# Audio tower with routed experts: all first weights resident, sums fetched by token number, tiles scattered into the output

## The chip, the cores and the metric

The kernel runs on one core of one Trainium2 chip. The time is the device time of one execution in microseconds (us), and lower is better. Times of the unchanged kernel are the median of three runs. The engines are named as in the profile: PE is TensorE (matmuls; PEld is its weight load), DVE is VectorE, ACT is ScalarE, POOL is GpSimd, SP is SyncE, which here only issues DMAs. A "q" behind an engine's name is its queue of instructions other than computing ones.

## What is computed

The input is 64 signals of 4000 samples. Seven strided convolutions of 128 channels, each with a layernorm over the channels and an exact gelu, leave 12 tokens for each signal, 768 tokens in all. A projection takes them to 192 values, an attention with 6 heads inside each signal of 12 tokens is added, and last a layer with 9 experts:

```
xt = layernorm(h).reshape(-1, 192)
route_prob = softmax(xt @ Ws + bs)
p, routes = max(route_prob), argmax(route_prob)
h1 = gelu(einsum('td,edf->tef', xt, W1) + b1)
out = einsum('tef,efd->ted', h1, W2) + b2
common = out[:, 0, :]
sel = out[token, routes[token], :]
final = where(routes == 0, common, p * sel + (1 - p) * common)
return h + final
```

W1 is 9 x 192 x 768, W2 is 9 x 768 x 192, all float32. Expert 0 is computed for every token (the common part). Experts 1 to 8 are computed only for the tokens that chose them.

## The kernel before

All five engines have a program of their own, written out by hand, and meet in semaphores. The signals are worked in 8 groups (`NT`) of 8. A table of slots (`SLOTS`, lines 121 to 218) sets which chunk of which convolution and which side job stands in a slot, and every engine walks that same table. The tokens of a group are worked 16 to 22 slots behind its last convolution (`STEP_AT`, `TIGHT`). The last slots (`DRAIN`) hold the last group's chunks, its attention and the common expert's jobs "up" and "down". Behind the table come `AFTER` = down(6), up(3), down(7).

What matters here is what follows the last convolution:

- **Choice.** For each group DVE finds the chosen expert and each token's place among that expert's tokens; POOL scatters the 96 rows, with the token's number as 193rd element, by an indirect DMA into the DRAM table `sorted_tokens` (line 623), which has a region for each expert. When the last group is placed, DVE works out in 13 short steps (lines 1255 to 1270) which expert owns each of the 13 tiles (`owni`) and at which row it starts (`rowi`). `s_own` tells of both.
- **Tiles.** `NTILE` is 13 and a tile is 128 rows. SP reads an owner and starts that expert's W1 and its row of b1 (lines 535, 536) into one of `WR` = 3 buffers: 576 KB. Two of these lie in the stream buffer h[1][0] and one in `xhl`. It then loads the tile's tokens (line 542) into one of `XR` = 4 buffers. Its order is weights 0 to 2, tokens 0 to 3, then weights j and tokens j+1 in turn. Weights j wait for up(j-3), and tokens j wait until tile j-4 is stored.
- PE turns the 128 x 192 tokens (lines 969, 970), multiplies with W1 (lines 981, 982: 24 instructions), and after ACT's gelu (line 1431) with W2 (line 993: 12 instructions). W2 of all experts lies in SBUF from early on. PE's order is turn(j+2), up(j+1), down(j). DVE copies the turned tokens (`take`, line 1292) and adds the chosen bias (`result`, line 1299). POOL stores the tile by an indirect DMA into the DRAM table `chosen_results` (line 696) and, before each store, waits for the one before it.
- **End.** When all tiles are stored, SP loads `chosen_results` back in four parts (line 557), DVE adds p times it to `acc` (line 1317, 8 instructions), and SP writes four parts of the output (line 561). `acc` holds h plus (1-p) times the common part; lines 1279 to 1312 make it between tiles 1 and 2.

W1 of expert 0 (`W1c`) is loaded at the start. The biases `b2s` are loaded by SP when the last convolution is done (line 527).

## Time and profile before

| | us |
|---|---|
| median of 3 runs | 646.53 (645.88 to 650.91) |
| the profiled execution, its own time | 646.93 |
| its span, first to last instruction | 645.1 |
| last convolution chunk starts on PE | 496.0 |
| last down job of the common expert ends on PE | 550.7 |
| first turn of a tile starts on PE | 555.0 |
| last result of a tile starts on DVE | 633.0 |
| busy in the span: PE, DVE, ACT, POOL | 569.5, 315.0, 301.8, 277.0 |

The profiled execution lies 0.4 us above the median, and 1.8 us of it lie outside the span. The page's busy shares are means over stages of different kinds: up to about 496 us the convolutions stream through all engines, from there to 551 us one group's attention and choice run as a chain of small steps, from 551 to 633 us the 13 tiles run, and the rest is the end. Only the last two stages and what feeds them are touched by the change, so a reader has to look at stretches and not at the totals.

### The profile page before, as it was taken

What the parts mean: (1) busy time and instruction counts of PE and PEld (TensorE: products, weight loads), DVE (VectorE), ACT (ScalarE), POOL (GpSimd) and SP (SyncE); (2) the same over time, 40 slices, a digit from 0 to 9 for tenths busy, and PEclk for the clock granted to TensorE, in tenths of its full rate; (3) what the DMA queues carried; (4) which work ended last, traced back from release to release, by engine and by line L of the source; (5) the groups of instructions that cost most, each with busy time, mean ns of one, the idle gap of its engine ahead of it and who ended that gap; (6) DMA issues with size and microseconds to landing.
All of it is one profiled execution on the core that took longest, in us unless ns stands there. A gap on an engine that the chain in (4) does not pass through costs nothing.

```text
span 645.1 us, 11944 instructions
## 1 busy us (share of the span) xinstructions
PE 569.5 (88%) x4499; PEld 538.3 (83%) x4499; DVE 315.0 (49%) x736; ACT 301.8 (47%) x494; POOL 277.0 (43%) x410
## 2 busy tenths in 40 slices
PE   6877899989989999998999999899997787687882
PEld 6776899989989989998998999889986666687882
DVE  4653465455657566665756666555544233131112
ACT  1545466746655674665567466546434132011110
POOL 4573285794267429526742952343322101011111
PEclk9998999999999999999999999999999756799997
DMA  6290000790000000000000000000001001544532
GB/s 181 71 269 9 3 1 10 170 228 24 2 1 10 8 1 1 6 1 2 1 6 2 1 7 1 1 1 6 2 6 54 6 1 43 133 103 108 142 105 85
DMA packets 19403, 29.21 MB, mean 45 GB/s; under 512 B 1916, under 2 KB 14567, under 8 KB 19349
## 3 DMA queue, kind: packets, MB, share of 16 engines
q1 hardware_dynamic: 16853, 19.97, 11.3%
q0 software_dynamic: 2480, 8.49, 5.5%
q8 instruction: 37, 0.61, 0.4%
q14 instruction: 17, 0.14, 0.1%
q10 hardware_dynamic: 16, 0.00, 0.0%
HBM read 19.38 MB, written 9.08 MB: 44 GB/s over the span
## 4 chain that ended last, share of the span: by engine, by line
PE 66%; POOL 8%; DMA 7%; ACT 7%; DVE 6%; issue 4%; SPq 1%; DVEq 0%; POOLq 0%; ACTq 0%
PE ps L738 36%; PE ps L750 5%; DMA chosen_results<-h 4%; PE ps L803 3%; POOL rstd L596 3%; POOL rstd L605 2%; PE ps L824 2%; DMA h<-sorted_tokens 2%; PE ps L993 2%; ACT h L1368 2%; ACT sq L1339 2%; PE ps L864 2%; PE ps L981 2%; PE ps L794 2%; PE ps L982 2%
## 5 line engine op out<-in xcount | busy, mean ns | idle before, releaser
L738 PE MATMUL ps<-wt,h 128*128 128x128 f32 (+2 forms) x2496 | 301.7, 276 | 16.0 <-ACT h L1368 9.0
L738 PEld LDWEIGHTS ps<-wt,h 128*128 128x128 f32 (+2 forms) x2496 | 290.9, 189 | 21.2 <-issue 13.1
L1339 ACT ACTIVATE sq<-ps 128x512 f32<-128x512 f32 (+7 forms) x128 | 67.3, 526 | 184.3 <-PE ps L738 184.0
L605 POOL TENSOR_TENSOR rstd<-varv,neghalf 128x4 f32<-128x4 f32 (+7 forms) x128 | 117.0, 914 | 10.0
L1068 DVE TENSOR_REDUCE ssum<-sq 128x4 f32<-128x512 f32 (+7 forms) x128 | 75.5, 590 | 87.5 <-ACT sq L1339 87.4
L1078 DVE TENSOR_TENSOR xh<-ps,rstd 128x512 f32<-128x512 f32 (+7 forms) x128 | 76.3, 596 | 82.8 <-POOL rstd L605 82.7
L1357 ACT ACTIVATE h<-ps,lncol 128x512 f32<-128x512 f32 (+7 forms) x128 | 112.8, 881 | 5.9 <-PE ps L750 5.3
L602 POOL TENSOR_TENSOR varv<-ssum,ceps 128x4 f32<-128x4 f32 (+7 forms) x128 | 26.2, 205 | 204.5 <-DVE ssum L1068 204.2
L596 POOL TENSOR_TENSOR rstd<-var,half 128x10 f32<-128x10 f32 (+2 forms) x39 | 82.8, 2131 | 9.4 <-DVE var L1034 9.4
L1368 ACT ACTIVATE h<-ps,lncol 128x512 f32<-128x512 f32 (+1 forms) x120 | 82.0, 727 | 2.2 <-PE ps L803 2.2
L750 PE MATMUL ps<-ident,xh 128*128 128x128 f32 (+2 forms) x424 | 66.3, 270 | 6.7 <-ACT h L1357 5.5
L750 PEld LDWEIGHTS ps<-ident,xh 128*128 128x128 f32 (+2 forms) x424 | 49.5, 141 | 9.6 <-issue 6.9
L696 POOL DMA_INDIRECT chosen_results<-h x13 | 12.5, 964 | 81.0 <-DVE h L1299 78.9
L803 PE MATMUL ps<-xcol,w0t 120*128 120x512 f32 (+1 forms) x120 | 43.3, 424 | 2.1 <-DVE xcol L1055 0.8
L1431 ACT ACTIVATE h<-ps 128x768 f32<-128x768 f32 x13 | 10.5, 811 | 70.9 <-PE ps L982 70.9
L1299 DVE TENSOR_TENSOR h<-ps,wt 128x192 f32<-128x192 f32 x13 | 4.7, 358 | 50.2 <-PE ps L993 50.2
L993 PE MATMUL ps<-W2s,h 128*128 x156 | 27.3, 326 | 0.0
L1055 DVE CAST xcol<-ps 120x512 fp32r<-120x512 f32 (+1 forms) x40 | 25.1, 628 | 1.4 <-PE ps L794 1.3
L993 PEld LDWEIGHTS ps<-W2s,h 128*128 128x128 f32 x156 | 25.1, 190 | 0.0
L824 PE MATMUL ps<-W2s,h 128*96 128x192 f32 x96 | 23.8, 415 | 0.4 <-ACT h L1374 0.4
L803 PEld LDWEIGHTS ps<-xcol,w0t 120*128 120x128 f32 x120 | 19.6, 190 | 5.2 <-ACT h L1368 2.5
L794 PE MATMUL ps<-ident,xhl 128*120 128x128 f32 x144 | 22.4, 273 | 1.3 <-DVE xhl L1048 1.2
(208 smaller groups left out, 655.8 us busy)
## 6 DMA issues: line engine op xcount, KB each, us to landing
sorted_tokens<-zero POOLq DMA_DIRECT2D x1, 5886.5 KB, 32.2
W2s<-in_L_ffn_W_dram SPq DMA_DIRECT2D x9, 576.0 KB, 8.4
h<-in_L_ffn_W_dram SPq DMA_DIRECT2D x9, 576.0 KB
xhl<-in_L_ffn_W_dram SPq DMA_DIRECT2D x4, 576.0 KB
h<-sorted_tokens SPq DMA_DIRECT2D x13, 96.5 KB, 2.0
xnat<-in_x_dram SPq DMA_DIRECT2D x7, 135.0 KB
wt<-in_L_ffn_b_dram SPq DMA_DIRECT2D x1, 864.0 KB, 4.0
h<-in_L_tok_conv_w_dram SPq DMA_DIRECT2D x4, 192.0 KB, 3.9
```

What stands on the lines that cost most here:

```text
L596: gp.tensor_tensor(rstd0[:, lo:hi], var0[:, lo:hi], half0[:, lo:hi], ALU.pow).then_inc(s_pow, 1)
L605: gp.tensor_tensor(rstd[0:rows, idx, 0:count], varv[0:rows, idx, 0:count], neghalf[0:rows, 0:count], ALU.pow).then_inc(rstd_done, 1)
L738: last = nc.tensor.matmul(y[0:rows, j * C:(j + 1) * C], src, wt[:, TAP0[l] + tap, :], start=(tap == 0), stop=(tap == taps - 1))
L750: last = nc.tensor.transpose(tr[:, j * rows:(j + 1) * rows], xh[0:rows, n % 2, j * C:(j + 1) * C], ident[0:rows, 0:rows])
L803: nc.tensor.matmul(o[:, 0:w], w0t[:, j, :], xcol[q % 2][0:12 * K0, 0:w], start=True, stop=True).then_inc(j_done, 1)
L824: last = nc.tensor.matmul(o[0:M, 0:D], hc[:, f, i * M:(i + 1) * M], W2s[:, 0, f, :], start=(f == 0), stop=(f == NF - 1))
L993: last = nc.tensor.matmul(o, ht[:, b, f * P:(f + 1) * P], W2s[:, bass.ds(own, 1), f, :].rearrange("p e d -> p (e d)"), start=(f == 0), sto ...
L1068: nc.vector.reduce_sum(ssum[0:rows, n % 4, 0:count], sq[0:rows, n % 2, 0:w].rearrange("p (j c) -> p j c", c=C), axis=X).then_inc(ssum_done, 1)
L1078: nc.vector.tensor_tensor(xh[0:rows, n % 2, 0:w].rearrange("p (j c) -> p j c", c=C), ybank(n)[0:rows, 0:w].rearrange("p (j c) -> p j c", c=C),
L1339: nc.scalar.activation(sq[0:rows, n % 2, 0:w], ybank(n)[0:rows, 0:w], ACT.Square).then_inc(sq_done, 1)
L1357: nc.scalar.activation(dst, src, ACT.Gelu, bias=lncol[:, 8 + l:9 + l], scale=lncol[:, l:l + 1]).then_inc(act_done, 1)
L1368: nc.scalar.activation(dst, src, ACT.Gelu, bias=lncol[:, 8:9], scale=lncol[:, 0:1]).then_inc(j_act, 1)
```

## The change

Six things, in the order of the program:

1. **Memory.** The stream buffers of the convolutions become one tensor `wide`, with W1 of expert 0 ahead of them. `W1s` is a view of it that holds W1 and b1 of all 9 experts. Buffers that lay in the stream buffers move: `ht` to `work` (which held `sq` and `xh`), `xs` to `cols` (which held `xcol`), `ysb` to `xnat`. `XR` is 5 and `YB`, the number of result and sum buffers, is 4.
2. **Weights.** Behind the last convolution SP loads W1 of experts 1 to 8 with 8 DMAs (4.6 MB) and b1 with two. The 13 loads by owner are gone.
3. **Pick.** For each tile ACT copies the owner's 97 x 1536 values from `W1s` to one of two buffers (`xhl`, `watt`), from which PE multiplies. The matmuls, their number and their shapes stay.
4. **Tokens.** SP loads tokens j when `take(j-5)` has copied that buffer's token numbers to `idt`.
5. **Common part.** DVE makes the shares and `acc` ahead of tile 0, around down(7), and not between tiles 1 and 2. `acc` has a 193rd element, p. POOL then writes `acc` to the DRAM table `common_sums` and its first 192 elements to the output, and fetches the first 4 tiles' rows of `common_sums` by token number.
6. **Result.** DVE multiplies the chosen bias by p and adds the fetched sum, and then adds p times PE's result to that: two instructions. `result(j-2)` stands behind `take(j+2)`. PE's down tile goes round three banks. POOL scatters the finished rows into the output itself (rows without a token are left out by the bounds check), waits only for the store four tiles back, and fetches the sums for tile j+4. The load of `chosen_results`, the last 8 additions and the output's four DMAs are gone, and so is the early DMA that cleared `chosen_results`; `common_sums` has its last 128 rows cleared instead.

```diff
+XR = 5
+YB = 4
+        wide = sb("wide", [P, 2 * DFF + 2 * sum(ODD[l] + EVEN[l] for l in range(1, 6))])
+        W1s = wide[0:DH + 1, 0:2 * DFF * NE].rearrange("p (e k c) -> p e k c", e=NE, k=2)
...
+        W1r = [xhl[:, :, :].rearrange("p l k -> p (l k)")[0:DH + 1, 0:2 * DFF], watt[:, :]]
...
# SP
             sp.dma_start(b2s, bass.AP(a["L0_ffn_b2"].tensor, 0, [[0, P], [1, NE * D]])).then_inc(s_b2, 16)
+            for e in range(1, NE):
+                sp.dma_start(W1s[0:DH, e, :, :], a["L0_ffn_W1"][e].rearrange("(k p) n -> p k n", p=DH)).then_inc(s_w1, 16)
+            for k in range(2):
+                sp.dma_start(W1s[DH:DH + 1, 1:NE, k, :], a["L0_ffn_b1"][1:NE, :].rearrange("(a e) n -> a e n", a=1)).then_inc(s_w1, 16)
             sp.wait_ge(s_own, 2)
+            sp.wait_ge(s_sent, 16 * NT)
...
                 if j >= XR:
-                    sp.wait_ge(s_ys[(j - XR) % 2], 16 * ((j - XR) // 2 + 1))
+                    sp.wait_ge(e_ids, j - XR + 1)
...
-            for i in range(0, NT, 2):
-                sp.dma_start(sel[:, i:i + 2, :], ys_dram[i * M:(i + 2) * M, :].rearrange("(i p) d -> p i d", p=M)).then_inc(s_got[i // 2], 16)
...
# POOL
+            def fetch_sums(j):
+                gp.wait_ge(e_ids, j + 1)
+                gp.indirect_dma_start(out=sums[:, j % YB, :], out_offset=None,
+                                      in_=sum_dram[:, :], in_offset=ids(j)).then_inc(s_got[j % YB], 16)
+            gp.wait_ge(c_acc, NT)
+            gp.dma_start(sum_dram[0:TOKENS, :].rearrange("(i p) d -> p i d", p=M), acc[:, :, :]).then_inc(s_sums, 16)
+            gp.dma_start(out_rows.rearrange("(i p) d -> p i d", p=M), acc[:, :, 0:D]).then_inc(s_out, 16)
+            gp.wait_ge(s_sums, 16)
+            for j in range(YB):
+                fetch_sums(j)
+            gp.wait_ge(s_out, 16)
             for j in range(NTILE):
                 gp.wait_ge(e_res, j + 1)
-                if j >= 1:
-                    gp.wait_ge(s_ys[(j - 1) % 2], 16 * ((j - 1) // 2 + 1))
+                if j >= YB:
+                    gp.wait_ge(s_ys[j % YB], 16 * (j // YB))
+                gp.indirect_dma_start(out=out_rows, out_offset=ids(j), in_=ysb[:, j % YB, :], in_offset=None,
+                                      bounds_check=TOKENS - 1, oob_is_err=False).then_inc(s_ys[j % YB], 16)
+                if j + YB < NTILE:
+                    fetch_sums(j + YB)
# DVE
+                ve.wait_ge(s_got[b], 16 * (j // YB + 1))
+                nc.vector.scalar_tensor_tensor(out=sums[:, b, 0:D], in0=b2s[:, bass.ds(own * D, D)], scalar=sums[:, b, D:D + 1],
+                                               in1=sums[:, b, 0:D], op0=ALU.mult, op1=ALU.add).then_inc(s_mix, 1)
...
+                nc.vector.scalar_tensor_tensor(out=ysb[:, b, :], in0=ps[:, 4 + j % 3, 0:D], scalar=sums[:, b, D:D + 1],
+                                               in1=sums[:, b, 0:D], op0=ALU.mult, op1=ALU.add).then_inc(e_res, 1)
...
                 if j + 2 < NTILE:
                     take(j + 2)
-                result(j)
+                if j >= 2:
+                    result(j - 2)
# ACT
+            def pick(j):
+                own = ac.value_load(owni[0:1, j:j + 1], min_val=0, max_val=NE - 1)
+                nc.scalar.copy(W1r[j % 2], W1s[:, bass.ds(own, 1), :, :].rearrange("p e k c -> p (e k c)")).then_inc(e_pick, 1)
+            ac.wait_ge(s_own, 1)
+            ac.wait_ge(s_w1, 16 * (NE + 1))
+            pick(0)
+            ac.wait_ge(t["at"], NT)
+            pick(1)
             for j in range(NTILE):
                 hidden(j)
+                if j + 2 < NTILE:
+                    pick(j + 2)
```

ACT's program, from its last common gelus to the end, before (h_0 and ps are the tile's hidden values and PSUM):

```order
L1374 ACTIVATE h<-ps 128x96 x6
L1431 ACTIVATE h_0<-ps 128x768 x13
L275 UNCONDITIONAL_BRANCH
```

and the same place now, with the two copies ahead of the first gelu and the first behind it (`wide` holds all experts' W1, `xhl` and `watt` the picked one):

```order
L1396 ACTIVATE h<-ps 128x96 x6
L1457 TENSOR_LOAD owni
L1457 ISA x2
L1458 ISA
L1458 COPY xhl<-wide 97x1536
L1457 TENSOR_LOAD owni
L1457 ISA x2
L1458 ISA
L1458 COPY watt<-wide 97x1536
L1453 ACTIVATE work<-ps 128x768
```

Between two gelus there now stand an owner's load and a copy of 1536 values a partition.

POOL's program from its last scatter of sorted tokens on, before:

```order
L623 DMA sorted_tokens<-xn,sloti 7808x193
L696 DMA chosen_results<-h_0 896x192 x13
L275 UNCONDITIONAL_BRANCH
```

and now, down to the third store:

```order
L620 DMA sorted_tokens<-xn,sloti 7808x193
L696 DMA common_sums<-acc 96x8x193
L697 DMA out_dram<-acc 96x8x192
L691 DMA h<-common_sums,idt 128x193 x4
L706 DMA out_dram<-xnat,idt 768x192
L691 DMA h<-common_sums,idt 128x193
L706 DMA out_dram<-xnat,idt 768x192
L691 DMA h<-common_sums,idt 128x193
```

Two whole stores and four fetches come ahead of the first tile's store, and a fetch stands behind each of the first nine.

SP's program at its end, before:

```order
L535 DMA h_0<-in_L_ffn_W_dram 96x2x768
L536 ISA
L536 DMA h_0<-in_L_ffn_b_dram 1x768
L557 DMA h<-chosen_results 96x2x192 x4
L561 DMA out_dram<-acc 96x2x192 x4
L275 UNCONDITIONAL_BRANCH
```

and now from the biases on, where the weights come ahead of the first tokens:

```order
L540 DMA wt<-in_L_ffn_b_dram 128x1728
L542 DMA wide<-in_L_ffn_W_dram 96x2x768 x8
L544 DMA wide<-in_L_ffn_b_dram 1x8x768 x2
L549 TENSOR_LOAD rowi
L549 ISA x2
L552 ISA
L552 DMA cols<-sorted_tokens 128x193
```

SP has nothing behind the last tile's tokens but the waits for the stores.

## Rows read from the trace of the kernel before

**Rows 1.** The chain that ended last, and waits from 550 us: total, times, longest.

```profile
PE 66%; POOL 8%; DMA 7%; ACT 7%; DVE 6%; issue 4%; SPq 1%; DVEq 0%; POOLq 0%; ACTq 0%
...
PE ps L969 <- DMA h<-sorted_tokens: 14.4, 10, 4.4
```

**Rows 2.** Stretches: length, busy us (count) of PE, PEld, DVE, ACT, POOL; clock, DMA share, GB/s.

```profile
551.00:560.80 9.80, 5.09 (x28) 4.72 (x29) 0.88 (x3) 0.00 (x0) 0.00 (x0) 0.65 0.38 94
560.80:633.00 72.20, 62.02 (x468) 59.04 (x467) 12.61 (x38) 10.54 (x13) 11.57 (x12) 1.00 0.42 110
```

**Rows 3.** Timeline of several engines, 496 to 569 us: start, length, engine, instruction.

```profile
496.59 0.37 SPq L527 DMA_DIRECT2D wt<-in_L_ffn_b_dram  x1
...
541.24 0.96 POOL L623 DMA_INDIRECT sorted_tokens<-xn,sloti  x1 [5.71 <-DVE sloti L1177]
...
548.10 0.25 ACT L1374 ACTIVATE h<-ps 128x96 f32<-128x96 f32 x1 [0.24 <-PE ps L815]
...
550.69 0.35 DVE L1059 TENSOR_TENSOR h<-ps,b2c 96x192 f32<-96x192 f32 x1 [5.94 <-PE ps L824]
...
555.01 0.42 PE L969 MATMUL ps<-ident,h 128*96 128x128 f32 x1 [4.35 <-DMA h<-sorted_tokens]
...
556.77 0.63 PE L981 MATMUL ps<-xst,h 96*128 96x128 f32 x2
...
563.76 2.12 PE L993 MATMUL ps<-W2s,h 128*128 x12
...
568.61 2.12 PE L993 MATMUL ps<-W2s,h 128*128 x12
```

**Rows 4.** Pieces of the chain that ended last: start, length, what.

```profile
543.84 0.48 SPq L531
...
544.83 0.35 SPq L535
...
557.40 0.43 PE ps L982 x2
...
567.17 2.38 DMA chosen_results<-h
...
569.71 1.97 DMA h<-sorted_tokens
...
572.15 0.22 PE ps L981 x2
...
574.83 1.97 PE ps L993 x12
```

**Rows 5.** Timeline of DVE, POOL and SP, 571 to 645 us.

```profile
571.15 0.21 DVE L1279 TENSOR_REDUCE r<-lgb 96x8 f32<-96x72 f32 x1
...
572.62 2.72 DVE L1312 SCALAR_TENSOR_TENSOR acc<-h,c,acc 96x192 f32<-96x192 f32 x8
...
631.09 0.36 DVE L1299 TENSOR_TENSOR h<-ps,wt 128x192 f32<-128x192 f32 x1 [4.27 <-PE ps L993]
...
633.04 0.36 DVE L1299 TENSOR_TENSOR h<-ps,wt 128x192 f32<-128x192 f32 x1 [1.59 <-PE ps L993]
...
637.15 1.81 SPq L557 DMA_DIRECT2D h<-chosen_results  x4
```

**Rows 6.** The chain's piece for the last but one store.

```profile
631.72 2.32 DMA chosen_results<-h
```

**Rows 7.** Groups on ACT by shape: count, busy us, mean ns, idle before.

```profile
L1396 ACT ACTIVATE t<-t 96x576 f32<-96x576 f32 x8 | 5.5, 684 | 0.1
...
L1431 ACT ACTIVATE h<-ps 128x768 f32<-128x768 f32 x13 | 10.5, 811 | 70.9 <-PE ps L982 70.9
```

**Rows 8.** DMA issues: engine, count, KB each, median us to landing.

```profile
sorted_tokens<-zero POOLq DMA_DIRECT2D x1, 5886.5 KB, 32.2
...
wt<-in_L_ffn_b_dram SPq DMA_DIRECT2D x1, 864.0 KB, 4.0
```

**Rows 9.** A stretch of PE: length, busy, granted clock, DMA share, GB/s.

```profile
505.00:506.00 1.00, 0.17 (x2) 0.55 0.00 0
```

More of the change, by code:

```diff
@@ L33 @@
 ROWS = (NE - 1) * REGION + NTILE * P
-WR = 3
-XR = 4
+XR = 5
+YB = 4
 SEG = 16
@@ L396, in audio_tower @@
         xs_dram = nc.dram_tensor("sorted_tokens", [ROWS, D + 1], F32, kind="Internal").ap()
-        ys_dram = nc.dram_tensor("chosen_results", [TOKENS + P, D], F32, kind="Internal").ap()
+        sum_dram = nc.dram_tensor("common_sums", [TOKENS + P, D + 1], F32, kind="Internal").ap()
+        out_rows = out.rearrange("b t d -> (b t) d")
         ps = ctx.enter_context(nc.psum_tensor("ps", [P, 8, 512], F32))
@@ L459, in audio_tower @@
         s_sent = sem("tokens_sorted")
-        s_w1 = [sem(f"first_weights_here{k}") for k in range(WR)]
+        s_w1 = sem("first_weights_here")
         s_xs = [sem(f"tile_tokens_here{k}") for k in range(XR)]
+        e_pick = sem("tile_weights_picked")
         e_turn = sem("tile_turned")
+        e_ids = sem("tile_numbers_kept")
         e_copy = sem("tile_copied")
@@ L1270, in _ @@
             nc.vector.tensor_copy(rowi[:, :], rowf[:, :]).then_inc(s_own, 1)
-            for job in AFTER:
-                if job[0] == "down":
-                    job_down(job)
             def shares():
```

126 lines of the change are left out of this document (60 added, 66 removed).

## The prediction

> **What bounds the kernel now.** I read the chain that ended last first. PE holds 66% of it, but that is a mean over the whole program [rows 1]. So I cut the end into stretches [rows 2]. Up to 551 us the change touches nothing on the chain; behind that come three parts.
>
> - From 551.0 to 560.8 us PE is busy 5.1 of 9.8 us at a mean clock of 0.65 [rows 2]. The last down job is taken by DVE at 550.69 to 551.04, but PE turns the first tile only at 555.01, after 4.35 us that end with a DMA of sorted tokens [rows 3]. SP had three experts' weights to issue ahead of the tokens: its owner is read at 543.84 and the first weights start at 544.83 [rows 4]. The tokens queue behind 1.7 MB.
> - From 560.8 to 633.0 us PE is busy 62.0 of 72.2 us at full clock [rows 2]. Ten times it waits for tokens, 14.4 us in all with the 4.4 us of the first [rows 1], so 10.0 us inside the loop. The chain tells why: store of a tile 2.38 us, then tokens 1.97 us [rows 4]. Tokens j wait for the store of tile j-4, which shares the DMA engines with 576 KB of weights.
> - Where tokens were in time, two tiles follow each other at PE's own pace: W2 matmuls start at 563.76 and 568.61 [rows 3], a period of 4.85 us. It is made of up, 2.68 us (572.15 to 574.83), down, 1.97 us [rows 4], and 0.2 us for the turn.
> - From 633.04 to the end at 645.1 us PE has nothing to do: result, two stores in a row, loads back at 637.15, additions, output [rows 5].
>
> **The change part by part**, against this execution's span of 645.1 us.
>
> *Weights early.* SP may start them at 496.59, where the biases go today [rows 3]. Price: 4.72 MB. The biases' 864 KB landed in 4.0 us and the clearing of 5886 KB in 32.2 us [rows 8], so 216 and 183 KB a us, or 22 to 26 us. They are in by 525 us, and ACT wants them at 548.35, the end of its last common gelu [rows 3]. 23 us are to spare. PE waits on small steps meanwhile, and only the scatters share the DMA engines, so I cost it at nothing. Upper end: 1 us, if the small scatters or the engines' instruction fetch are held up.
>
> *Start of the tiles.* SP can issue the first tokens 1.0 us after 543.84 [rows 4]; 1.97 us later they are there, at about 547. The last scatter starts at 541.24 [rows 3] and is in before. Even at twice that price the tokens are early, so what is late next is down(7) on DVE, 551.04. DVE's new work ahead of it: down(6), shares, seven additions. From 571.15 to 572.62 seven of the short steps take 1.5 us and eight additions 2.72 us [rows 5]; now eight steps and seven additions, 1.7 + 2.4 = 4.1 us, start at about 544.7 and end at 548.8, before the down job. The eighth addition, 0.35 us, lies beside PE's first turn. So turn 0 starts at 551.15. Today 1.76 us lie between it and up(0) (555.01 to 556.77) at half clock [rows 3]; at full clock I take 1.35. up(0) starts at 552.5, not 556.77.
>
> *Clock of up(0).* Two matmuls took 0.43 us in it, and 0.22 us later on [rows 4]. Now PE pauses only 0.5 us before the turns, not 4.35. I take full clock: up(0) ends at 555.2 and the first W2 matmul starts 2.9 us later (turn, up(1)), at 558.1, against 563.76. That is 5.65 us saved.
>
> *Pick.* An ACT copy of 1536 values from SBUF stands nowhere in this trace. 576 values from SBUF took 0.684 us and 768 from PSUM 0.811 [rows 7]. Scaled by length alone these give 1.8 and 1.6 us; with a fixed part of 0.2 us, 1.4 to 1.5. Bounds 1.4 and 1.9; I take 1.5. The owner's load before it costs 1.0 us at most, as on SP [rows 4]. Ready: 548.35 + 2.5 = 550.9 for tile 0, before 552.5; 553.4 for tile 1, before 555.4. In the loop ACT has 0.81 + 1.0 + 1.5 = 3.3 us of work in 4.85. The tightest is tile 2: its copy waits for up(0)'s end, 555.2, is ready at 558.6, and PE wants it at 560.3. PE hides it; without cover it costs its excess over 1.7 us once, and over 1.5 us on each tile.
>
> *Sums.* The last addition ends at 551.45. POOL issues two stores of 0.59 MB, an issue 0.9 to 1.0 us as for the scatter [rows 3]. At 183 KB a us [rows 8] each moves in 3.2 us; with 2 us until it is noticed, `common_sums` is whole at about 558, at the latest 561 where both share. The first fetch lands 2.4 to 4 us on, at 560 to 565. Who waits: `result(0)` stands behind `take(4)`, at about 565; behind it stand `take(5)`, for which PE asks at 574.7, and PE's down(3) at 572.6. So 7 us are to spare for PE. Nothing is added.
>
> *Loop.* DVE per tile: take, number copy, two additions of 0.41 at most [rows 5], an owner's load of 1.0 us: 2.5 us. POOL: a store and a fetch, 0.96 each plus 0.3 before each: 2.5 us. Tokens now wait for a copy of numbers five tiles back, 20 us early. All lie under 4.85. From 558.1: ten periods, 48.5; one without turn, 4.65; the last two downs, 3.95. End of PE at 615.2. Today the same takes 563.76 to 633.0, 69.3 us; now 57.1. That is 12.15 us saved.
>
> The Trainium skill has a rule that speaks against this (SBUF — State Buffer, section 'SBUF: two separate sides'): a VectorE operation with two SBUF inputs and a GpSimd operation that reads SBUF take a port pair in turn and block each other for a whole instruction. The new bias addition is such a one. By that rule DVE's 2.5 us grow by up to 0.96 to 3.5, and POOL's by 0.4; the sum stays and the third rival gets a little more. The trace has additions of that kind beside no DMA issue, so it shows nothing of it.
>
> *End.* Today 12.05 us behind 633.04. Now: the last addition 0.41, 0.3 to the store (631.09 + 0.36 to 631.72 [rows 5, 6]), the store 2.32 [rows 6], and 0.4 for the closing of the engines: 3.4 us. POOL's former wait for the store before is gone. 8.65 us saved.
>
> **Sum.** 5.65 + 12.15 + 8.65 = 26.45. Span 645.1 - 26.45 = 618.65, and 1.8 us outside it: 620.5 us for such an execution. This one lay 0.4 us above the median of 646.53; I leave that for the small costs taken as nothing. Forecast 620.5.
>
> **Rivals.**
>
> 1. *The clock falls at the seam or inside the loop.* For: it went down around 505 us in a pause of about 2 us (mean 0.55 in that stretch) [rows 9], and PE has two pauses of about 0.5 us at the seam. Against: in the loop pauses of 1.0 us a tile left it at 1.00 throughout [rows 1, 2]. Price: up(0) and part of up(1) at half clock, as from 556.77 on: 1.3 us, to 2.9 if the turns and a whole further round go slow. 620.5 + 2.5 = 623 us. The Trainium skill (TensorE: Matmul & The Clock Gate, section 'A second HAM failure mode: psum-queue depth-cycling') says that short idle times between groups of matmuls can make the clock swing; by that rule this rival would be likelier than the loop's 1.00 makes it.
> 2. *The sums are late.* If the store of 0.59 MB took as long as the large clearing, 32.2 us [rows 8], they would be there at 584, the first rows at 587, and PE, stopped at 572.6, would lose 15 us: 636 us. Against: the clearing moved ten times the bytes.
> 3. *A helper becomes the bound of a tile.* ACT, if a copy takes over 3.0 us with its load at 1.0, or DVE with loads and blocked ports. At half a us over on each of 13 tiles: 627 us. Against: the upper bound of 1.9 us from [rows 7] leaves 1.1 us.
> 4. *Slower than before.* Each store and fetch on POOL is generated by that engine. If a fetch of 128 rows of 772 B costs far more than the scatter's 0.96 us [rows 3], POOL sets the pace. It takes 26.5 us over 13 tiles, so 4.85 + 2.04 = 6.9 us a tile, to reach today's time: a fetch of over 5.3 us. At 6 us the time is 656 us. For: no gather stands in this trace. Against: a scatter of rows as long is the same work the other way.
>
> **How the numbers follow.** Forecast 0.72 (618.5 to 622.5 by its own bounds: copy, closing, seam), rival 1 0.12, rival 3 0.08, rival 2 0.05, rival 4 0.03. The range goes from 618.0, where the small steps turn out cheaper, to 626.5: it takes in rival 1 and part of 3 and leaves out some 0.15. A measurement of this kernel tells from no change about 1%, 6.5 us. Rivals 1 to 3 are all faster than that, so faster 0.96, within 1% 0.01, slower 0.03.
>
> **What would show it.** Right: first turn at about 551.2 us with no wait for tokens; PE's W2 groups 4.85 us apart throughout, clock 1.00 from there on; ACT's copies near 1.5 us; PE's last matmul at about 615 us and the end under 4 us behind; weights landed by 525 us. Wrong: PE waiting for the pick, a mean clock under 0.9 from 551 to 561 us, DVE waiting for fetched sums past 566 us, POOL's fetches well over 1 us, or a longer stretch from 500 to 551 us, where the weights now move.

## The result and the profile after

The changed kernel took 627.02 us (median of four runs, 622.12 to 628.29) where the kernel before, on the same chip, took 648.72 us (645.88 to 651.43). The ratio is 0.966, interval 0.962 to 0.970. The forecast was 620.5 us in a range of 618.0 to 626.5, so the sign and most of the size came out, and the median lies 0.5 us above the range. Five later runs of the same program on another occasion (E1) gave 621.99 us and a ratio of 0.961.

The profiled execution took 628.29 us, with a span of 626.6 us and a mean granted TensorE clock of 0.953. Its span against that of before and the prediction, cut at four places that all traces have. The third row, from the last down job of the common expert to the first W2 matmul of a tile, is called the seam below:

| stretch | before | predicted | after | E1 |
|---|---|---|---|---|
| start to SP's load of the biases (last convolution done) | 496.59 | 496.59 | 501.52 | 497.65 |
| to DVE's last common down job | 54.10 | 54.10 | 54.19 | 51.81 |
| to the first W2 matmul of a tile | 13.07 | 7.41 | 7.37 | 7.36 |
| to DVE's last result | 69.28 | 57.10 | 57.54 | 57.50 |
| to the end | 12.06 | 3.45 | 5.98 | 5.98 |
| span | 645.1 | 618.65 | 626.6 | 620.3 |

Each number is the start of a row minus the start of the row before it: before, 496.59, 550.69, 563.76 and 633.04 us [rows 3, 5]; after, 501.52, 555.71, 563.08 and 620.62 us, all shown below. Two of the five rows differ from what was predicted: the first, by 4.9 us, and the last, by 2.5 us. Together with 0.5 us in the loop they make the 8 us by which the span is longer than forecast.

The chain's shares by engine, from the page of the profile after, and PE's longest waits (total, times, longest):

```profile
PE 74%; POOL 8%; ACT 7%; DVE 6%; issue 4%; DMA 1%; SPq 1%; POOLq 0%; DVEq 0%; ACTq 0%
...
PE ps L750 <- ACT h L1390: 9.0, 5, 2.7
```

Against [rows 1] DMA fell from 7% of the chain to 1%. The wait for tokens, 14.4 us before, is gone from the list; the longest that PE has now are for ACT's gelus in the head of the program, the convolutions' part up to the load of the biases, which will matter below.

The two stretches of [rows 2], in the columns given there:

```profile
551.00:560.80 9.80, 8.17 (x63) 7.48 (x62) 4.63 (x16) 4.52 (x8) 1.67 (x2) 0.99 0.45 110
...
560.80:615.00 54.20, 54.20 (x428) 53.84 (x428) 14.39 (x45) 24.61 (x23) 22.63 (x23) 1.00 0.22 61
```

PE is busy 54.20 of 54.20 us where it was busy 62.0 of 72.2, and the mean clock of the first stretch is 0.99, not 0.65. The share of the DMA engines in the loop fell from 0.42 to 0.22.

The timeline of after from the end of the convolutions on, the places of [rows 3]:

```profile
501.52 0.37 SPq L540 DMA_DIRECT2D wt<-in_L_ffn_b_dram  x1
501.93 4.40 SPq L542 DMA_DIRECT2D wide<-in_L_ffn_W_dram  x8
...
551.37 2.39 DVE L1305 SCALAR_TENSOR_TENSOR acc<-h,c,acc 96x192 f32<-96x192 f32 x7
...
554.04 1.47 ACT L1458 COPY xhl<-wide 97x1536 f32 x1 [0.67 <-issue]
...
555.71 0.35 DVE L1071 TENSOR_TENSOR h<-ps,b2c 96x192 f32<-96x192 f32 x1 [1.95 <-PE ps L836]
...
556.17 0.28 PE L981 MATMUL ps<-ident,cols 128*96 128x128 f32 x1 [0.49 <-issue]
...
557.14 0.88 POOL L696 DMA_DIRECT2D common_sums<-acc  x1 [9.92 <-DVE acc L1305]
...
557.50 0.39 PE L993 MATMUL ps<-xst,xhl 96*128 96x128 f32 x2
...
563.05 1.04 POOL L691 DMA_INDIRECT h<-common_sums,idt  x1 [4.25 <-DMA common_sums<-acc]
...
563.08 2.12 PE L1005 MATMUL ps<-W2s,work 128*128 x12
...
567.93 2.12 PE L1005 MATMUL ps<-W2s,work 128*128 x12
...
571.33 0.42 DVE L1312 SCALAR_TENSOR_TENSOR h<-wt,h 128x192 f32<-128x192 f32 x1 [0.56 <-issue]
```

Read from top to bottom: the weights start when the convolutions end; DVE's seven additions take 2.39 us and are over at 553.76, 1.95 us before the last common job; ACT's copy takes 1.47 us and is done at 555.51, before PE asks for it at 557.50; PE turns the first tile 0.46 us after that last job started on DVE, where it used to turn it 4.32 us after it; and the W2 groups lie 4.85 us apart. The fetched sums are issued at 563.05 and used at 571.33, with nobody waiting.

The end of after: the timeline of DVE and POOL, the last pieces of the chain (start, length, what), and the closing of POOL's program (durations in ns, start):

```profile
620.62 0.42 DVE L1318 SCALAR_TENSOR_TENSOR xnat<-ps,h 128x192 f32<-128x192 f32 x1 [1.00 <-PE ps L1005]
621.83 0.98 POOL L706 DMA_INDIRECT out_dram<-xnat,idt  x1 [1.21 <-DVE xnat L1318]
```

```profile
621.07 0.03 POOLq L706
621.10 0.51 issue
621.61 1.21 POOLq L275
```

```profile
L275 POOLq DRAIN  x1: 4715/4715/4715, 621.6 to 621.6; - x1
```

The store starts 0.79 us behind the result, and not the 0.27 of before. Then POOL's closing instruction, which begins at 621.61, ends only at 626.33, 3.5 us behind the end of the store's issue at 622.81. That is the end of the program. In the trace of before the same instruction is there too:

```profile
L275 POOLq DRAIN  x1: 3718/3718/3718, 634.6 to 634.6; - x1
```

It began at 634.58 and ended at 638.30, 2.5 us behind the issue that ran from 634.80 to 635.76. The reload of the results lay over it, so it cost nothing, and the prediction, which allows 0.4 us for the closing of the engines, did not count it.

### The profile page after: what moved, and what is told of

Read it like the earlier page. It is cut to its first block, busy times and chain, and to the rows that moved or that the text cites. A ratio compares the mean times of both kernels' runs of the same rounds, so it can differ in the third digit from the quotient of the medians.

```text
span 626.6 us, 11944 instructions
## 1 busy us (share of the span) xinstructions
PE 572.0 (91%) x4499; PEld 542.5 (87%) x4499; DVE 319.8 (51%) x755; ACT 320.0 (51%) x507; POOL 291.6 (47%) x425
## 4 chain that ended last, share of the span: by engine, by line
PE 74%; POOL 8%; ACT 7%; DVE 6%; issue 4%; DMA 1%; SPq 1%; POOLq 0%; DVEq 0%; ACTq 0%
PE ps L750 38%; PE ps L762 5%; PE ps L1005 4%; PE ps L836 3%; PE ps L815 3%; POOL rstd L593 3%; PE ps L994 3%; PE ps L993 3%; POOL rstd L602 2%; ACT h L1390 2%; ACT work L1361 2%; PE ps L876 2%; PE ps L806 2%; ACT wide L1379 2%; PE ps L896 1%
## 5 line engine op out<-in xcount | busy, mean ns | idle before, releaser
L750 PE MATMUL ps<-wt,h 128*128 128x128 f32 x1248 | 155.3, 282 | 10.0 <-ACT h L1390 9.0
L1361 ACT ACTIVATE work<-ps 128x512 f32<-128x512 f32 (+7 forms) x128 | 67.3, 525 | 188.4 <-PE ps L750 188.1
L750 PEld LDWEIGHTS ps<-wt,h 128*128 128x128 f32 x1248 | 150.2, 198 | 11.8 <-issue 6.5
L750 PE MATMUL ps<-wt,wide 128*128 128x128 f32 (+2 forms) x1248 | 150.5, 274 | 5.6 <-ACT wide L1379 5.4
L750 PEld LDWEIGHTS ps<-wt,wide 128*128 128x128 f32 (+2 forms) x1248 | 144.6, 184 | 9.0 <-issue 6.1
L1080 DVE TENSOR_REDUCE ssum<-work 128x4 f32<-128x512 f32 (+7 forms) x128 | 75.6, 590 | 91.6 <-ACT work L1361 91.5
L1090 DVE TENSOR_TENSOR work<-ps,rstd 128x512 f32<-128x512 f32 (+7 forms) x128 | 76.4, 597 | 82.8 <-POOL rstd L602 82.7
L1379 ACT ACTIVATE wide<-ps,lncol 128x512 f32<-128x512 f32 (+6 forms) x120 | 109.3, 911 | 2.3 <-PE ps L762 1.6
L762 PE MATMUL ps<-ident,work 128*128 128x128 f32 (+2 forms) x424 | 66.9, 272 | 6.5 <-ACT wide L1379 5.5
L762 PEld LDWEIGHTS ps<-ident,work 128*128 128x128 f32 (+2 forms) x424 | 50.2, 143 | 9.1 <-issue 6.9
```

What stands on the lines that cost most here:

```text
L750: last = nc.tensor.matmul(y[0:rows, j * C:(j + 1) * C], src, wt[:, TAP0[l] + tap, :], start=(tap == 0), stop=(tap == taps - 1))
L762: last = nc.tensor.transpose(tr[:, j * rows:(j + 1) * rows], xh[0:rows, n % 2, j * C:(j + 1) * C], ident[0:rows, 0:rows])
L1080: nc.vector.reduce_sum(ssum[0:rows, n % 4, 0:count], sq[0:rows, n % 2, 0:w].rearrange("p (j c) -> p j c", c=C), axis=X).then_inc(ssum_done, 1)
L1090: nc.vector.tensor_tensor(xh[0:rows, n % 2, 0:w].rearrange("p (j c) -> p j c", c=C), ybank(n)[0:rows, 0:w].rearrange("p (j c) -> p j c", c=C),
L1361: nc.scalar.activation(sq[0:rows, n % 2, 0:w], ybank(n)[0:rows, 0:w], ACT.Square).then_inc(sq_done, 1)
L1379: nc.scalar.activation(dst, src, ACT.Gelu, bias=lncol[:, 8 + l:9 + l], scale=lncol[:, l:l + 1]).then_inc(act_done, 1)
```

## The experiments

Times are medians over the executions of a kernel; stretches and rows are those of its one profiled execution. The ratio is always to the kernel before, run on the same chip in the same session.

### E1: the changed kernel again

> The changed kernel unchanged, five rounds. Theory (the 6.5 us by which the forecast was missed are 4.9 us of TensorE's clock ahead of the change's stages and 2.5 us of the end): single runs fall into steps, about 622 us where the mean granted clock is 0.968, 626 at 0.960, 628 at 0.953, so time falls with the clock, some 0.4 us for each 0.001, and kernel before shows the same steps (646 to 651). Rival (the moved buffers or the early weights cost 5 us in every execution): times of the changed kernel do not follow the clock, and no run is below 624.

Measured: 621.99 us (five runs, 620.75 to 623.38, clock 0.965 to 0.971) against 647.46 us in the same session, ratio 0.9614 (0.9584 to 0.9643). The rival, no run below 624 us, is out. Over all nine executions the time goes with the clock, as the theory has it: 628.2 and 628.3 us at 0.953, 625.85 at 0.960, 623.4 at 0.965, 622.0 to 622.1 at 0.968, 620.8 to 620.9 at 0.971. The table above has its stretches. The three that the change is about agree with those of after within 0.04 us; the first two are 3.9 and 2.4 us shorter. So the same program varies by 6 us between these two profiles, and all of it lies ahead of the seam. The next runs ask whether TensorE's clock makes this difference.

### E2 and E3: the three pauses of the head filled, in the changed kernel and in the one before

```diff
+HEADFILL = {(1, 0, 5): 7, (1, 1, 0): 7, (1, 1, 1): 8}
...
+            def fill(k, bank):
+                for _ in range(k):
+                    nc.tensor.matmul(ps[:, bank, 0:P], ident[:, :], ident[:, :], start=True, stop=True)
             def conv(chunk):
...
+                if chunk in HEADFILL:
+                    fill(HEADFILL[chunk], n % 3)
```

> The changed kernel with 7, 7 and 8 matmuls without use put into the three pauses of PE at 42 to 64 us (ahead of chunks (1,0,5), (1,1,0), (1,1,1)); each takes about 0.22 us at full clock, 1.5 to 1.8 us in a pause of 2.2 to 2.7. Theory: the clock stays at 1.00 from 45 to 70 us, the 4 us lost there come back, times gather at 621 to 624 us with less spread. Rival (it isn't the pause): clock and times as without them, 622 to 628, or up to 1 us longer where the fill outlasts a pause.

> The same three fills in the kernel before. Theory: 640 to 645 us, less spread than 645.9 to 651.4, and the difference to the filled changed kernel is 23.5 to 24.5 us (26.45 as predicted, less 2.5 of the end). Rival: times as before, 646 to 651.

PE has three pauses of 2.2 to 2.7 us near 45, 55 and 64 us. The convolution of 24 matmuls behind each of them shows the clock by its length. Timeline of PE, before, and then after:

```profile
45.34 2.92 PE L738 MATMUL ps<-wt,h 128*128 128x128 f32 x24 [2.36 <-ACT h L1368]
...
54.23 4.54 PE L738 MATMUL ps<-wt,h 128*128 128x128 f32 x24 [2.18 <-ACT h L1368]
...
62.57 2.92 PE L738 MATMUL ps<-wt,h 128*128 128x128 f32 x24 [2.65 <-ACT h L1368]
```

```profile
44.83 4.43 PE L750 MATMUL ps<-wt,h 128*128 128x128 f32 x24 [2.35 <-ACT h L1390]
...
55.35 4.54 PE L750 MATMUL ps<-wt,h 128*128 128x128 f32 x24 [2.19 <-ACT h L1390]
...
63.69 5.46 PE L750 MATMUL ps<-wt,h 128*128 128x128 f32 x24 [2.66 <-ACT h L1390]
```

The pauses are the same in both, and the work too. Before, one of the three convolutions ran for the most part at the lower of the clock's two levels (1.2 and 2.4 GHz); after, all three. Set against before at the same instruction of POOL, after is 0.5 us early at 44 us, 3.7 us late at 67 us and still 3.7 us late at 493 us. The last 1.2 us of the 4.9 come just ahead of the load of the biases, where after's clock is 0.50 to 0.53 from 497 to 500 us: four matmuls of 288 columns (L826, L827 of after) take 2.05 us there, and 1.32 before. The stretch from 15 to 70 us (length, then busy us of PE, PEld, DVE, ACT, POOL, clock, DMA share, GB/s), in after, and then in E2:

```profile
15.00:70.00 55.00, 44.18 (x298) 40.82 (x297) 25.64 (x60) 26.44 (x39) 27.31 (x24) 0.88 0.37 107
```

```profile
15.00:70.00 55.00, 48.44 (x387) 44.91 (x386) 27.95 (x63) 29.14 (x43) 29.44 (x28) 1.00 0.37 108
```

Measured: E2 620.85 us (618.84 to 621.93), ratio 0.960 (0.957 to 0.963), just under the 621 to 624 expected; E3 644.69 us (641.43 to 647.5, twelve runs), ratio 0.995 (0.993 to 0.998). With the pauses filled the clock from 15 to 70 us is 1.00 in E2, and its load of the biases starts at 494.06 us, against 501.52 in after. In the four profiled executions with filled pauses (E2, E3, E4, E10) all twelve convolutions take 2.94 us; in the ten without, 21 of 30 take 4.2 to 5.5 us. What follows: the head of the changed kernel is not slower as such; unfilled, it ended between 496.24 and 501.66 us in the nine profiled executions of kernels with the new layout (after, E1, E5, E6, E8, E9, E11 to E13), and before's 496.59 lies near the lower end of that.

Filling is worth about 1 us to E1's median and 3 us to the median before. It does not remove the whole spread of the head. An earlier place, from 17 to 27 us, was left unfilled in every run: PE pauses twice for 0.83 us there, and the clock from 15 to 30 us is 0.77 in E4 and E8, 0.89 in E1, E3 and E5, and 1.00 in the other nine. E4's head therefore ends at 497.03 us, though its three convolutions are at full clock, and E3's at 495.76.

The difference of the medians of E3 and E2, where neither has a slow convolution at 45 to 64 us, is 23.8 us, inside the 23.5 to 24.5 expected. The three stretches of the table, 5.70 + 11.74 + 6.08, make 23.5 of it; those of E3 and E2 themselves make 23.2.

### E4 and E10: the later pauses filled as well

E4 keeps the fills of the head and adds unused matmuls to eight steps of the last group between 500 and 541 us. E10 leaves out one of these steps (turn_norm_h) and adds one more of the last group (scores), two of the group before, the last common up job and the first turns.

```diff
 # E4
+LATEFILL = {'turn_norm_h': 5, 'turn_1': 6, 'turn_probs': 5, 'values': 3, 'turn_heads': 1, 'turn_2': 8, 'logits': 1, 'rank': 4}
...
+                if r == NT - 1 and step in LATEFILL:
+                    fill(LATEFILL[step], 0)
 # E10
+LATEFILL = {('turn_2', 6): 6, ('rank', 6): 6, ('turn_1', 7): 6, ('scores', 7): 1, ('turn_probs', 7): 5, ('values', 7): 3, ('turn_heads', 7): 1, ('turn_2', 7): 8, ('logits', 7): 1, ('rank', 7): 4}
...
+                if (step, r) in LATEFILL:
+                    fill(LATEFILL[step, r], 0)
...
+                if job == ("up", 3, 2):
+                    fill(5, 0)
...
+            fill(2, 0)
             pe.wait_ge(j_dve, DVE_TO[len(JOBS)])
             turn_tile(0)
+            fill(2, 0)
```

> The changed kernel with the head filled and, for the last group alone, 1 to 8 matmuls without use ahead of eight steps for which PE waits (500 to 551 us, where the clock is at half for most of the time). Theory: the clock stays high in more of that stretch, the last group's chain of PE pieces shortens by 5 to 12 us: 611 to 618 us. Rival (the fills outlast the pauses at half clock and the clock falls all the same): 0 to 5 us longer than the head filled alone.

> The changed kernel with matmuls of two 128 x 128 identity tiles, whose results nobody reads, put into every pause of PE that the trace shows as long: the three in the head, the chain of small steps of the last two groups, the last common up job, and the start of the tiles. The output is unchanged. My theory is that what is left of the spread (620.8 to 623.4 us of the same program) is the granted clock, so with the pauses filled the time should be about 615.5 us (614 to 618) with a mean clock over 0.985, under e4's 618.34 because e4 still had low stretches at 500 and 541 us. The rival, that the low clock is not tied to PE's pauses, gives 618 to 622 us with low stretches at the same places. If the unused matmuls themselves delay work on the chain, the times would not fall under e4's fastest, 614.87 us, though the clock is full.

E4 gave 618.34 us (614.87 to 622.64), ratio 0.955 (0.952 to 0.958), 0.3 us above the 611 to 618 expected. Its profiled execution, the slowest of the six, had a low stretch from 541.2 to 554.9 us that reaches across the seam into the first up. In the other profiled executions that have the new layout and their tokens in time, the first up runs at full clock. Window and one matmul pair of the first up:

```profile
541.20:554.90 13.70, 12.07 (x49) 10.54 (x49) 3.59 (x13) 3.78 (x5) 2.70 (x3) 0.50 0.46 130
```

```profile
549.10 0.63 PE L1004 MATMUL ps<-xst,xhl 96*128 96x128 f32 x2
```

So rival 1 of the prediction exists: the first up at half clock. From the last common job (546.88) to the first W2 matmul (557.45) E4 took 10.57 us, against 7.37: 3.2 us, a little over the upper end of 2.9 that the rival was given. What PE did before the fall: it paused for 1.31 us ahead of 539.11, worked on, and from 541.16 its matmul pairs take 0.63 to 0.70 us and not 0.36 to 0.46.

The rule of the Trainium skill that stood beside that rival (TensorE: Matmul & The Clock Gate, section 'A second HAM failure mode: psum-queue depth-cycling'), that short idle times between groups can make the clock swing, is borne out at one place: behind the two pauses of 0.83 us at 17 to 21 us the same convolution takes 4.68 us in E4 and 2.84 in after. The loop, at 1.00 in all kernels with tokens in time, gives no sign of it, and the falls at 45 to 64 us stand behind longer pauses.

E10 gave 611.94 us (610.48 to 616.03), ratio 0.946 (0.941 to 0.950), the fastest version of all: 10 us under E1, with the output unchanged. Its windows:

```profile
496.00:541.70 45.70, 39.25 (x275) 35.97 (x276) 20.29 (x75) 14.16 (x28) 4.91 (x10) 0.93 0.51 136
541.70:606.90 65.20, 63.46 (x496) 62.64 (x495) 17.14 (x52) 26.18 (x25) 26.65 (x28) 1.00 0.22 61
```

The stretch from the biases' load to the last common job takes 46.44 us (494.43 to 540.87) where after took 54.19, and its clock is 0.93 instead of the 0.65 in this row of after:

```profile
501.50:555.70 54.20, 40.75 (x187) 35.55 (x187) 20.39 (x75) 13.69 (x29) 5.64 (x12) 0.65 0.45 115
```

The seam, the loop and the end stay at 7.34, 57.30 and 5.99 us. I had expected 615.5, so the fills were worth 3.6 us more than I gave them. They take no wait away, so what they work on is the clock. The length of the same stretch goes with its mean clock in these profiles: 54.1 to 54.3 us at 0.65 (before, after, E2, E12), 51.8 to 52.2 at 0.70 or 0.71 (E1, E6, E13), 49.85 at 0.84 (E4), 46.44 at 0.93. What these later fills would give the kernel before was not run.

### E5: tokens wait for the store again

```diff
                 if j >= XR:
-                    sp.wait_ge(e_ids, j - XR + 1)
+                    sp.wait_ge(s_ys[(j - XR) % YB], 16 * ((j - XR) // YB + 1))
```

> The changed kernel, but tokens j wait again for the store of tile j-5 and not for the copy of its token numbers. Theory (the wait on the store made the stops of the loop, and late results make it worse): from the first turn of tile k+4 on, DVE's two additions, 0.9 us to the store, 2.4 us for it and 2.1 us for the tokens make 7.4 us against a period of 4.85, so 2.5 us on each of 8 tiles: 642 us, and PE waits for tokens. Rival (only the weights' traffic made the stops): 622 us as without it.

Measured: 645.84 us (642.97 to 648.71), ratio 0.995 (0.992 to 0.999). PE's wait for tokens is back, and the chain shows one turn of the loop:

```profile
PE ps L981 <- DMA cols<-sorted_tokens: 14.8, 7, 3.0
```

```profile
594.46 2.08 DMA cols<-sorted_tokens
...
598.25 0.43 DVE xnat L1318
...
598.74 0.77 issue
599.51 3.02 DMA out_dram<-xnat,idt
```

The loop takes 80.0 us (559.87 to 639.88), longer than the 69.3 of before although the weights' traffic is gone and the store waited for is one tile older. By the chain, the reason is the new order on DVE: a result now comes two tiles behind its turn, so its store is later by as much. The old order with the new weights, E9 below, takes 61.39 us in the loop. The two edits belong together: without the wait for the copied numbers the delayed results would have cost 22.5 us in the loop. Waits of up to 3 us also took the clock down inside the loop (0.51 from 604 to 611 us), which is part of it; the expectation was 642.

### E6: the weights only when the owners are known

```diff
+            sp.wait_ge(s_own, 2)
             for e in range(1, NE):
...
-            sp.wait_ge(s_own, 2)
             sp.wait_ge(s_sent, 16 * NT)
```

> The changed kernel, but SP starts the 4.7 MB of weights only when the owners are known, and not at the last convolution. Theory (the early place hides 20 us of transfer): weights start at about 544 instead of 502 us (by a profile whose first tile turns at 551), land 19 to 20 us on, the first up tile starts near 567 instead of 552.5: 637 us; the stretch up to 545 stays the same within 0.5 us, since early weights cost nothing there. Rival (early weights slow the attention of the last group): that stretch gets 1 us or more shorter.

Measured: 644.2 us (641.47 to 650.98), ratio 0.995 (0.990 to 1.000), 7 us more than I had said. ACT waits for the last weights, and PE for tokens queued behind them. Timeline of ACT and of PE, and the window of the low clock:

```profile
566.27 0.42 PE L981 MATMUL ps<-ident,cols 128*96 128x128 f32 x1 [17.72 <-DMA cols<-sorted_tokens]
...
566.74 1.47 ACT L1458 COPY xhl<-wide 97x1536 f32 x1 [20.49 <-DMA wide<-in_L_ffn_b_dram]
```

```profile
552.60:573.00 20.40, 5.92 (x26) 5.15 (x27) 0.96 (x4) 2.84 (x2) 2.02 (x2) 0.50 0.74 212
```

From DVE's last common job (548.59) to the first W2 matmul (576.27) it is 27.7 us, 20.3 more than in E1. 17.2 of them are the longer wait for tokens (17.7 against 0.5 us), and 3.1 come from half clock in the first two up jobs (566.27 to 576.27 is 10.0 us, against 6.91 in after). With its weights loaded late the kernel gives back 22 of 25.5 us. The early transfer itself costs the stretch that it lies beside nothing that shows at equal clock: 54.19 us with it (after) and 54.10 without (before), both at 0.65, and 52.13 with it (E13) and 52.24 without (E6), both at 0.71.

### E9: memory, early weights and pick alone

The kernel before with parts 1 to 3 of the change; tokens, common part, result and end as they were.

```diff
+            for e in range(1, NE):
+                sp.dma_start(W1s[0:DH, e, :, :], a["L0_ffn_W1"][e].rearrange("(k p) n -> p k n", p=DH)).then_inc(s_w1, 16)
...
-            for j in range(WR):
-                load_weights(j)
             sp.wait_ge(s_sent, 16 * NT)
-            for j in range(XR):
+            for j in range(NTILE):
                 load_tokens(j)
-            for j in range(WR, NTILE):
-                load_weights(j)
-                if j + 1 < NTILE:
-                    load_tokens(j + 1)
...
+            def pick(j):
+                own = ac.value_load(owni[0:1, j:j + 1], min_val=0, max_val=NE - 1)
+                nc.scalar.copy(W1r[j % 2], W1s[:, bass.ds(own, 1), :, :].rearrange("p e k c -> p (e k c)")).then_inc(e_pick, 1)
```

> The kernel before with the new memory layout, the early weights and the pick alone; results, waits, stores and end are the old ones. Theory (both the weights' traffic and the wait on the store made the loop's stops): the seam's 5.65 us come, and of the loop's 12.1 some 7.5, since the chain result 0.46, 0.27 to the store, store 2.38 without traffic, 0.16, tokens 1.97 is still 0.5 us over the period of 4.85 on 9 or 10 tiles: 634 us against 647.5. Rival A (the weights' traffic was all of it): 630 us. Rival B (only the waits count): 642 us.

Measured: 634.91 us (632.0 to 636.98), ratio 0.977 (0.971 to 0.983), where the theory had 634 and the rivals 630 and 642. Stretches: 7.37 us at the seam, 61.39 in the loop, 11.8 at the end. PE's wait for tokens fell from 14.4 us to this:

```profile
PE ps L970 <- DMA cols<-sorted_tokens: 2.5, 4, 0.9
```

So the 11.7 us of the loop divide into 7.9 for parts 1 to 3, with the traffic of weights gone, and 3.85 for parts 4 to 6, of which PE's waits for tokens that hung on the store are 2.5. The rest, the additions that part 5 moved out of the loop among it, was not divided. The seam's 5.7 us come from parts 1 to 3, and the end's 6 us from parts 5 and 6.

### E11 and E12: the pick done twice and three times

```diff
             def pick(j):
                 own = ac.value_load(owni[0:1, j:j + 1], min_val=0, max_val=NE - 1)
+                for i in range(2):
+                    nc.scalar.copy(W1r[j % 2], W1s[:, bass.ds(own, 1), :, :].rearrange("p e k c -> p (e k c)")).then_inc(e_again, 1)
+                    ac.wait_ge(e_again, 2 * j + i + 1)
                 nc.scalar.copy(W1r[j % 2], W1s[:, bass.ds(own, 1), :, :].rearrange("p e k c -> p (e k c)")).then_inc(e_pick, 1)
```

The diff is E12's; E11 has one further copy in place of two.

> ACT copies the owner's weights twice for each tile, the second time behind the first, so the pick costs 2.95 us and not 1.47. ACT then has 0.81 + 2.95 + about 0.5 = 4.3 us of work in the 4.85 us of a tile, and the weights of tile 2, wanted 2.4 us after they are there in e1, are ready about 1 us too late at most. If PE hides the pick, as the prediction has it, the time stays at e1's 622.0 us within 1 us (621.0 to 623.5), and the distance of two W2 groups stays 4.85 us. If the copy were on the path, each of 13 tiles would pay 1.5 us: 641 us.

> Three copies for each tile: ACT's work is 0.81 + 4.42 + 0.5 = 5.7 us, over the 4.85 us of PE. Now ACT must set the pace: a period of 5.6 to 5.8 us in eleven tiles, some 9 us, and 1 to 3 us at the start, where the first two tiles' weights come late: 622.0 + 12 = 634 us (631 to 637). The point from which a copy decides is then between two and three times its size, as rival 3 of the prediction has it (a copy over 3.0 us with its load). The rival, that PE hides nothing of the pick, gives 660 us here and 641 us in e11.

E11: 622.4 us (621.61 to 628.19), ratio 0.961 (0.957 to 0.966): the second copy costs nothing, and the loop takes 57.30 us. E12: 628.62 us (626.2 to 633.25), ratio 0.972 (0.966 to 0.978). Timeline of ACT in E12, one tile:

```profile
563.89 0.80 ACT L1454 ACTIVATE work<-ps 128x768 f32<-128x768 f32 x1
564.60 2.97 ACT L1460 COPY watt<-wide 97x1536 f32 x2
567.60 1.47 ACT L1462 COPY watt<-wide 97x1536 f32 x1
568.97 0.80 ACT L1454 ACTIVATE work<-ps 128x768 f32<-128x768 f32 x1
```

ACT has no gap any more and its period is 5.08 us, 0.23 over PE's 4.85, so it is the bound. The loop takes 59.97 us, 2.5 more than E1's, which is 11 times 0.23, and the seam 10.08, 2.7 more, as the first two picks come late. I had put the period at 5.6 to 5.8 us and the time at 634, since I added half a us for the owner's load and the gaps between instructions. The rows show that the load adds nothing: the first copy starts 0.1 us before the gelu ahead of it has ended, and the gelu 0.1 us before the last copy has. Between the copies, each of which waits for the one before, 0.03 us pass. The point from which the pick decides is thus about 4.2 us of copying (three copies, 4.4 us, less the 0.23 us by which they exceed the period), and not the 3.0 us of rival 3.

### E8 and E13: what the end consists of

E8 stores the last tile's rows without the bounds check, into a table of their own; E13 lets SP store them there with a plain DMA. Both leave the last tile's rows out of the output.

```diff
 # E8, on POOL
+                if j == NTILE - 1:
+                    gp.indirect_dma_start(out=res_dram[:, :], out_offset=ids(j), in_=ysb[:, j % YB, :], in_offset=None).then_inc(s_ys[j % YB], 16)
+                    continue
...
 # E13, on SP, with POOL's loop one tile shorter
+            sp.wait_ge(e_res, NTILE)
+            sp.dma_start(res_dram[0:P, :], ysb[:, (NTILE - 1) % YB, :]).then_inc(s_last, 16)
```

> The changed kernel, but the last tile's rows go to a DRAM table of their own with no bounds check, so they are missing in the output. Theory (the bounds check costs the 0.8 us between a result and its store, against 0.3 in the kernel before, and a part of POOL's closing): from the end of the last addition to the store's start 0.3 us, POOL's closing ends 2.5 us behind the issue and not 3.5: 1 to 1.5 us less behind PE's last matmul, 6.0 to 4.6 us. Rival (it is the addressing by a copied number and the closing is what it is): both stay, 6.0 us.

> SP stores the last tile's 128 rows with one plain DMA into a table of their own, which leaves these rows out of the output; POOL's last software-generated DMA is then the store of tile 11, which in e1 starts at 613.39 us. Theory: POOL's closing hangs 3.5 us behind the end of its last DMA issue, whatever engine ends last. Then POOL closes at 614.4 + 3.5 = 617.9 us of a span like e1's 620.3, SP's store is seen at about 617.3, and the time falls by 2.4 us to 619.6. Rival: the closing is a fixed 2.4 us behind the moment at which the last wait for a store is over. Then the end is 617.3 + 2.4 = 619.7 us of the span and the time falls by 0.6 us only, to 621.4.

E8: 623.24 us (619.96 to 625.25), not to be told from E1's 621.99 by its time. By its trace the end is 5.4 us and not 5.98: the store starts 0.27 us behind the result, as in before, and POOL's closing is 3.5 us behind the issue as in after. So of the 1 to 1.5 us expected, 0.5 came, and the closing doesn't depend on the check. E8 changes the table written to as well as the check; before, which writes a third table with no check, has the same 0.27 us, so the check is the likelier cause of the 0.5 us, though the two were not parted.

E13: 619.65 us (618.63 to 625.59), ratio 0.960 (0.954 to 0.966). Timeline of DVE and SP, and the closing of POOL:

```profile
613.03 0.42 DVE L1323 SCALAR_TENSOR_TENSOR xnat<-ps,h 128x192 f32<-128x192 f32 x1 [0.76 <-PE ps L1010]
...
613.52 0.34 SPq L561 DMA_DIRECT2D own_results<-xnat  x1
```

```profile
L275 POOLq DRAIN  x1: 4632/4632/4632, 612.1 to 612.1; - x1
```

SP's store is in by 615.2 us, but the span ends at 616.9, when POOL's closing of 4.63 us, begun at 612.1, is over. POOL's last issue ran from 612.29 to 613.27, so that is again 3.5 us behind it; the rival, 2.4 us behind the last wait for a store, would have ended it at 617.6. The theory holds: the closing hangs on the end of POOL's own program, whose last work is an indirect DMA, and not on the last wait of another engine. Whether it counts from that DMA or from the program's end, these runs don't tell. The end became 3.9 us instead of 5.98. Why the closing lies 2.5 us behind the issue in before and 3.5 us in the changed kernels stays open. E9, which has parts 1 to 3 only, shows 2.5 us as before, so the difference comes with parts 4 to 6; neither the bounds check (E8) nor the tensor written to accounts for it.

## Why the prediction was right or wrong

- **Weights early**: right. Issued from 501.93 behind the biases, they keep the DMA engines full until about 524.5 us, 22.6 us with the biases' 0.88 MB among them; the 22 to 26 us were worked out for the weights alone. The clause "I cost it at nothing" held: at equal clock no cost shows (E6).
- **Start of the tiles** and **clock of up(0)**: right. 7.37 us from DVE's last common job to the first W2 matmul, against 7.41 worked out: the saving is 5.70 us against 5.65. That the clock held at the seam was likely and not sure: in E4 it did not. DVE's eight steps and seven additions took 1.68 + 2.39 us against 1.7 + 2.4.
- **Pick**: right. 1.47 us against 1.5, hidden, with a margin that E11 and E12 show to be larger than I gave it (two copies of 1.47 us cost nothing, three cost 0.23 us a tile; the load runs under the gelu).
- **Sums**: right in what matters. `common_sums` landed 5.7 us after its issue at 557.14 and was seen at 563.05. After's trace runs 5.0 us behind before's at this place, so that is the "about 558" of the prediction. The first fetch landed 2.6 us on, DVE used it at 571.33 and PE waited for nothing. A fetch takes 0.97 us of POOL, as the scatter does, so rival 4 fell with its premise. The port rule of the Trainium skill (SBUF — State Buffer, section 'SBUF: two separate sides'), weighed against the change, shows nowhere: the new bias addition takes 0.42 us on all 13 tiles, against the 0.41 us worked out for it. Only two of the 13 lie beside a DMA issue of POOL (612.28 and 614.92 us), so these two are all that speaks against the rule here.
- **Loop**: right but for 0.4 us. 57.54 against 57.1, that is 11.74 saved against 12.15. 0.24 us of the difference lie in the last two W2 groups, 4.31 us in after and 4.07 in E11, where the last gelu starts 0.9 us sooner behind its up. E9 divides the gain. E5 shows that the tokens' wait for the store has to go once the results come late; in the old order it cost 2.5 us (E9), the weights' traffic more.
- **End**: the step that failed; its mechanism was right and the term for the closing mis-sized. It read "0.3 to the store ... the store 2.32 ... and 0.4 for the closing of the engines: 3.4 us". Measured: 0.42 for the addition, 0.79 to the store, 0.98 for its issue, 3.52 for POOL's closing behind that and 0.3 for the last semaphores, 6.0 us. So 6.1 us were saved, not 8.65. No row stood behind the 0.4. Without these 2.5 us the median of 627.02 would have been 624.5, inside the range. The closing stood in the trace of before, under the reload that the change removed; the question "what is late next" was asked of each wait and not of this one. The bounds check in the new store was named in the change and given no price: 0.5 us.
- **Small costs, and the range**: the second step that failed is "Up to 551 us the change touches nothing on the chain", taken as meaning that this part would last as long. The change indeed touches nothing there, but that part varies by 5 to 6 us from execution to execution with the granted clock (E1 to E3, and the stretches under E10). The profiled execution of before happened to have one slow convolution of three in the head, that of after three. Rival 1 spoke of the clock only at the seam and inside the loop and priced it at 2.5 us; the head, with three pauses of more than 2 us, had none. With the end at its true size the forecast would have been 621.2 + 1.8 = 623.0, and E1's 621.99 and the first 627.02 both lie within some 4 us of that; a range that took in the head's clock would have reached from 618 to 629. That E1's median lies inside the range and near 620.5 is in part luck: the end's 2.5 us are made up for by a stretch behind the convolutions that was 2.3 us shorter than before's.
- The mechanism, in sum, was right in each part that the change touches, with the one term of the end too small: 645.1 - 5.70 - 11.74 - 6.08 = 621.6 us, and 4.9 us of clock ahead of the load of the biases and 0.1 us behind it make the 626.6 of the trace.

## What to carry to other kernels

When a change takes away the last work of a program, look in the trace for what ended unseen beneath it, above all the closing instruction of the engine that issued indirect DMAs, and price the new end from there. Before giving a range, read the granted clock of stretches that the change does not touch: where matmuls of one shape differ in length between rows that stand behind pauses of PE, the same program can come out some us longer next time. And on a chain of small dependent steps, unused matmuls in PE's pauses can be worth as much as a removed wait: here 10 us of 622.

## What was not expected of the hardware

- POOL's closing ends 2.5 us (before, E9) or 3.5 us (after, E1, E8, E13) behind its last indirect DMA's issue, while in after SP, which waits for that DMA, goes on at 624.0 us, 1.2 us behind the issue's end at 622.81.
- An indirect store with a bounds check starts 0.79 us behind the instruction that releases it; without one, 0.27 us (before, and E8 with another table).
- The same pause of 2.2 to 2.7 us of PE is followed by half clock in some executions and by full clock in others: the convolution behind it takes 2.92 us, or 4.2 to 5.5 us. With the other low stretches ahead of the last convolution's end this moved the end of the head between 496.2 and 501.7 us.
- After 17.7 us of waiting (E6) the low clock lasted some 7 us into the renewed work, 566.3 to 573.0 us.
- A weight copy on ACT of 97 x 1536 values takes 1.47 us and begins about 0.1 us before the instruction ahead of it ends, unless it waits for that one (E12: 0.03 us behind it).
